# Cross attention on one core: the lower part of the turned context ahead of the step's maxima on VectorE, and the turn of step 6 between values and queries

## The reference, cut to what matters

```python
def _L0_xattn_ref(query, key, value, Wq, bq, Wk, bk, Wv, bv, Wo, bo, ln_gamma, ln_beta):
    q = (query @ Wq + bq).reshape(b, sq, 16, 64)      # query: layernorm of x, (64, 64, 256)
    k = (key @ Wk + bk).reshape(b, sk, 16, 64)        # key = value = ctx, (64, 256, 256)
    v = (value @ Wv + bv).reshape(b, sk, 16, 64)
    scores = jnp.einsum('bqhd,bkhd->bhqk', q, k) / 8
    attn = jax.nn.softmax(scores, axis=-1)
    out = jnp.einsum('bhqk,bkhd->bqhd', attn, v).reshape(b, sq, 1024)
    out = out @ Wo + bo + residual
    return layernorm(out) * ln_gamma + ln_beta        # x = x + this
```

## Time and profile before

| | us |
|---|---|
| three runs | 2171.08, 2171.07, 2169.53 |
| median | 2171.07 |
| the profiled execution, whole | 2171.83 |
| its span, first to last instruction | 2170.1 |
| TensorE busy | 2109.5 (97%) |
| VectorE busy | 1576.1 (73%) |
| ScalarE busy | 1275.5 (59%) |
| GpSimd busy | 951.1 (44%) |
| granted TensorE clock, mean | 0.993 |

### The profile page before, as it was taken

How to read it: one execution, slowest core, us unless ns; L and a number is a source line. 1 busy time by engine, 2 the same in 40 slices (tenths; PEclk the granted TensorE clock), 3 DMA queues, 4 the chain that set the end, 5 groups by cost and what they waited for, 6 DMA issues and landing times.

```text
span 2170.1 us, 46318 instructions
## 1 busy us (share of the span) xinstructions
PE 2109.5 (97%) x15864; PEld 1851.0 (85%) x15865; DVE 1576.1 (73%) x2833; ACT 1275.5 (59%) x3067; POOL 951.1 (44%) x813
## 2 busy tenths in 40 slices
PE   8999999999999999999999999899998999999997
PEld 7898888898888888888888888677776888888886
DVE  7667767767767677677677676689996887666665
ACT  5566666656656665666656556477775335555553
POOL 5223322322333332233223323388885234777775
PEclk9999999999999999999999999999999999999999
DMA  4000000010010010000100100245533222333332
GB/s 154 11 21 25 22 22 24 10 34 19 14 34 19 14 34 14 19 24 13 31 24 10 34 10 1 81 140 152 152 121 100 88 78 54 54 53 53 54 55 42
DMA packets 100686, 103.91 MB, mean 48 GB/s; under 512 B 11952, under 2 KB 90160, under 8 KB 100624
## 3 DMA queue, kind: packets, MB, share of 16 engines
q1 hardware_dynamic: 86992, 84.47, 12.6%
q0 software_dynamic: 13632, 18.62, 5.3%
HBM read 72.52 MB, written 30.54 MB: 47 GB/s over the span
## 4 chain that ended last, share of the span: by engine, by line
PE 59%; DVE 17%; issue 9%; POOL 9%; ACT 3%; DMA 2%; DVEq 0%; POOLq 0%; SPq 0%; ACTq 0%
PE banks L915 33%; PE banks L958 6%; PE banks L988 5%; PE banks L1016 5%; POOL out_dram L2393 4%; PE banks L1003 3%; POOL r_x L2357 3%; DVE top L678 2%; DVE q_st L658 2%; DMA out_dram<-r_y,index 2%; PE banks L2232 2%; POOL index L2364 2%; DVE peak L675 2%; DVE s_peak L1550 1%; DVE s_rsum L1596 1%
## 5 line engine op out<-in xcount | busy, mean ns | idle before, releaser
L915 PE MATMUL banks<-ctxT_hi,qk_hi 128*128 128x256 f32 x1024 | 300.8, 294 | 0.0
L915 PE MATMUL banks<-ctxT_hi,qk_lo 128*128 128x256 f32 x1024 | 289.8, 283 | 0.0
L915 PE MATMUL banks<-ctxT_lo,qk_hi 128*128 128x256 f32 x1024 | 287.4, 281 | 0.0
L547 ACT ACTIVATE probs<-banks,nbias 128x256 f32<-128x256 f32 x512 | 236.0, 484 | 83.7 <-DVE nbias L680 83.3
L436 POOL TENSOR_TENSOR rinv<-rsum,inverse 128x4 f32<-128x4 f32 x96 | 96.7, 1008 | 408.3 <-ACT probs L547 408.3
L554 ACT ACTIVATE pc<-banks 128x512 f32<-128x512 f32 x256 | 153.0, 598 | 191.0 <-PE banks L915 187.9
L638 DVE TENSOR_TENSOR qk_lo<-banks,qk_hi 128x512 fp32r<-128x512 f32 x256 | 163.4, 685 | 88.0 <-ACT qk_hi L509 88.0
L675 DVE TENSOR_REDUCE peak<-banks 128x4 f32<-128x1024 f32 x128 | 156.3, 1221 | 90.6 <-PE banks L915 90.4
L915 PE MATMUL banks<-pT_hi,ctx_hi 128*128 128x512 f32 x512 | 205.2, 401 | 1.7 <-DVE pT_lo L638 1.7
L638 DVE TENSOR_TENSOR pT_lo<-banks,pT_hi 128x512 fp32r<-128x512 f32 x256 | 165.5, 684 | 56.7 <-ACT pT_hi L509 56.2
L915 PE MATMUL banks<-pT_hi,ctx_lo 128*128 128x512 f32 x512 | 202.3, 395 | 0.0
(11 more groups left out here) (273 smaller groups left out, 6195.1 us busy)
## 6 DMA issues: line engine op xcount, KB each, us to landing
ctx_raw<-in_ctx_dram SPq DMA_DIRECT2D x64, 256.0 KB, 2.7
experts_w<-in_L_ffn_We_dram SPq DMA_DIRECT2D x24, 512.0 KB, 4.0
x_in<-in_x_dram SPq DMA_DIRECT2D x16, 256.0 KB, 2.8
x_again<-in_x_dram SPq DMA_DIRECT2D x16, 256.0 KB, 2.8
x_stream<-z SPq DMA_DIRECT2D x16, 256.0 KB, 2.1
s_x<-x_stream SPq DMA_DIRECT2D x32, 128.0 KB, 3.8
s_x_again<-x_stream SPq DMA_DIRECT2D x32, 128.0 KB, 2.1
x_normalised<-s_xl SPq DMA_DIRECT2D x32, 128.0 KB, 1.7
```

The source lines that it names most:

```text
L547: nc.scalar.activation(probs[:, s % 2, p, :], scores[:, s % 2, p // 2, (p % 2) * SK:(p % 2 + 1) * SK], ACT.Exp, bias=nbias[:, s % 2, p:p + ...
L915: last = nc.tensor.matmul(out, a, b, start=(n == 0), stop=(n == 3 * len(pairs) - 1))
```

## The change

The order in which the work on the turned context stands is changed. Nothing is computed otherwise, and no instruction is added but those that reckon a semaphore's value.

- On VectorE, in steps 4, 5 and 7, `ctx_lower` is issued ahead of `peaks`.
- In step 6, `ctxT` moves on all engines: on TensorE and in the ring from ahead of xT to between v 1 and q 0; on ScalarE from ahead of `xT_upper` to behind the eviction of v 0 and ahead of `exps`; on VectorE from ahead of `xT_lower` to behind it. The ring of step 6 is then xT, v 0, v 1, ctxT, q 0, q 1, pc 0, pc 1, pt 0, pt 1: q 0 takes over the bank of xT, q 1 that of v 0, pc 0 that of v 1, pc 1 that of ctxT, and pt 0 and pt 1 those of q 0 and q 1 as before.

```diff
@@ ring_order
-        if half == 1 and g.next:
+        if half == 1 and g.next and b != 2:
             out.append(("ctxT", b))
         if s == 6 and g.next:
             out.append(("xT",))
         if b == 2 and (g.cur if half else g.prev):
             out += [("v", half, j) for j in range(2)]
+        if s == 6 and g.next:
+            out.append(("ctxT", b))
@@ scalar
-                if half == 1 and g.next:
+                if half == 1 and g.next and b != 2:
                     ctx_upper(g, b)
...
                     last.then_inc(free, 1)
+                if s == 6 and g.next:
+                    ctx_upper(g, b)
                 if g.cur and s in (2, 3, 6):
                     exps(g, s)
@@ vector
+                if half == 1 and g.next and b != 2:
+                    ctx_lower(g, b)
                 if g.cur:
                     peaks(g, s)
...
-                if half == 1 and g.next:
-                    ctx_lower(g, b)
                 if s == 6 and g.next:
                     xT_lower(g)
+                    ctx_lower(g, b)
@@ tensor
-                if half == 1 and g.next:
+                if half == 1 and g.next and b != 2:
                     do_ctxT(g, b)
                 if s == 6 and g.next:
                     do_xT(g)
                 if b == 2 and (g.cur if half else g.prev):
                     do_v(g, half)
+                if s == 6 and g.next:
+                    do_ctxT(g, b)
```

## The result

| | before | changed |
|---|---|---|
| median of five runs each, us | 2171.08 | 2182.16 |
| their range | 2169.53 to 2173.85 | 2180.9 to 2183.76 |
| ratio, 95% interval | | 1.0047, 1.0035 to 1.0058 |
| profiled execution, whole | 2171.83 | 2183.76 |
| its span | 2170.1 | 2182.0 |

The changed kernel is slower by 11 us in the medians and by 0.47% in the ratio; forecast were 7.5 us. The last row is worked out from the timelines: the start of the maxima of step 3 in group 15 less that in group 1, over 14. A group became 0.60 us longer, 0.5 was forecast; the 14 groups make 8.3 us, 15 would make 8.9.

What follows compares the result with a forecast made beforehand. TensorE's waits were taken to bound the kernel. A net loss of 0.5 us in each of 15 groups, 7.5 us, added to the median 2171.07 gave 2178.6 us, with a range of 2174 to 2186.

Steps and rivals of the forecast that it cites:

- the port: Rival, chance 0.10: resid of step 4 is held by GpSimd, costing 0.8 to 0.93 us per group, 2183 to 2185.
- What bounds: Whole loop: TensorE is busy 84.36 of a group's 84.67 us, so only its waits change the time.
- Step 5, the gain: In step 5 pt 1 no longer waits for ctxT_lo on TensorE; 0.36 us gained per group.
- Step 4, the price: ctxT_lo ahead of the maxima makes pT_lo 1.06 us late, delaying pc of step 5; 0.06 lost per group.
- Maxima of step 5: VectorE's maxima start later, but `top` is no longer held and the bias is ready as before; no cost.
- Step 6, the loss: The later turn delays ScalarE's exponentials, then q_st and pt 1; 0.5 us per group net, bounds 0.45 and 0.57.
- VectorE in step 6: The lower part ahead of v 1's eviction is no trouble, since pc 0 takes that bank later; no cost.
- Step 7: Moving the maxima back there costs nothing, as VectorE waits for the output projection; without that cover 1.06 at most.
- xT_lo: Rival, chance 0.10: 0.25 of the 0.39 before the queries is a true wait; loss 0.25 per group, 2174.8 us.
- Faster: Rival, chance 0.13: ScalarE's order ahead of the queries does not matter; only 0.30 gain per group stays, 2166.6 us.

Runs made afterwards that it cites:

- the swap of two lines: The changed kernel with ScalarE's exponentials of step 6 put ahead of the upper part of the turned context; group 84.58 us, median 2171.42 us, ratio 0.9994 against before.

## Why the prediction was right, step by step

The direction, the place of each wait and the range were right; the best value, 2178.6, was 3.6 us too low. Of that 1.4 are the group (15 times 0.10), and the rest has the size of the opening's spread, which no term of mine stood for. By the time alone luck was needed: 2182.16 lies nearer to the 2183 to 2185 of the port than to my 2178.6, and only the trace tells the two apart.

- **What bounds** was right: TensorE by its waits. Its busy time did not change by more than 0.1 in a group.
- **Step 5, the gain**: right in place and sign, mis-sized a little. The stall was worth 0.41 (84.65 to 84.24), not 0.36. I had measured it to the start of the first transpose behind the wait. From pt 0 to the next scores it was 1.21 (672.80 to 674.01) and is 0.79 (680.69 to 681.48), which is 0.42, just the wait of the weight load in the earlier trace rows. I had written that the rest of the 0.42 hides under matmuls in the pipeline; it did not.
- **Step 4, the price**: this term was the worst sized, 0.20 for 0.06. The 1.06 by which pT_lo would be late was right (1.04 against the turn of step 5 in the changed trace). Wrong was to take 0.05 from its end to the weight load "as at ctxT_lo": it was 0.21, since more waits stand between this one and the matmul. The kernel with the waits of pc last shows 0.15 of it.
- **Maxima of step 5**: right. `top` took 0.16 where it had taken 1.66, and the bias came 0.16 later than it had against the turn of step 5 (3.47 for 3.31), which cost nothing.
- **Step 6, the loss**: right in mechanism. From the first matmul of the queries to the first q_st it was 1.74 before and is 2.57 now (688.99 to 691.56): 0.83 late, with 0.75 and 0.87 as my bounds. The pause of 0.39 stands ahead of the turn now, as the upper bound had it; I took the middle. With a net gain of 0.23 in this trace instead of 0.30 that makes 0.60 per group instead of 0.5, just above my upper bound of 0.57.
- **VectorE in step 6** was right for this kernel, v 1 was evicted by 691.38, ahead of pc 0. I had not seen that the same queue is the next in line, once ScalarE's is cleared.
- **The port**: out. `resid` took 0.75 for its two instructions, as before, from 677.53 on, inside `rinv` (677.32 to 678.33). The Trainium skill ("SBUF — State Buffer", section "Who interferes with whom") has such an instruction blocked by any GpSimd instruction that reads SBUF. This trace disagrees for the small power instruction, and agrees for the large scaling, under which `top` of step 6 still takes 1.66.
- **Step 7** was right: its edit was put at nothing, and the way from its scores to the next took 15.60 for 15.58.
- **xT_lo**: out. It now ends 0.6 ahead of the queries, and the pause of 0.39 has gone to the turn, put down to issue. It goes with the end of the values and not with a wait for xT_lo.
- **Faster**: out. It needed 0.7 to 0.9 us of slack on ScalarE, and the swap of two lines gave 0.67 back.

## What to carry to other kernels

When an item is moved on one engine, look at what stands behind it in the queue of every other engine that handles it: here four transposes, moved behind the values, left ScalarE idle for 1.46 us with the exponentials behind them in its queue, and the queries paid. A stall that is removed uncovers the small delays that it had taken up; cost them at their full size then. Where a wait is likely to be the last, let the matmul itself carry it.

## What the runs showed of the hardware

- With a wait of TensorE written ahead of two other waits, each with a semaphore value to be reckoned, it took 0.21 us from the releaser's end to the weight load of the matmul behind them; written last, it took 0.05.
- After the values, whose weights are 64 columns wide, the next load of 128 columns came after 0.39 of idle in the records, for queries (681.53 and 723.43 before) and for transposes (688.57 in the changed kernel) alike.
- A VectorE instruction with two SBUF operands is held by GpSimd's 128x1024 multiplication until it ends (`top` 1.66 us instead of 0.16), and is not held by its 128x4 power instruction (`resid`, 0.75 for two, inside `rinv`).
- The opening of this kernel, the first 60 us with the weight loads, differs by 3.2 us between two executions of the same kernel and by up to 4.3 over the ten traces, more than some of the edits here are worth; within a trace the length of a group repeats within 0.09.
